# A fused two-layer cross-attention kernel: one engine's order in the first attention, and where the last two batches of the second attention are normalised

## What is computed

```
x = x + att0(layernorm(x), ctx)     # 16 heads of 16; + ctx and a second layernorm inside
x = x + moe(layernorm(x))           # 8 experts, the best 2 of each row, gated, 512 wide
x = x + att1(layernorm(x), ctx)     # 16 heads of 64; 77 text keys with relative positions
x = x + ffn(layernorm(x))           # 8-bit rounded rows, 1024 wide, depthwise convolution of 3

# att1, for one batch:
sim   = (q @ k_text + q @ rel_k[dist]) * scale        # dist = clip(j - i, -16, 16) + 16
attn  = softmax(sim)
out   = attn @ v_text + sum_j attn[i, j] * rel_v[dist[i, j]]
out  += softmax(q @ k_img) @ v_img * (tanh(alpha) + 1) + softmax(q @ k_aud) @ v_aud * (tanh(beta) + 1)
return out @ Wo + bo
```

## Time and profile before

| | |
|---|---|
| median of 3 runs | 952.82 us (952.13 to 952.98) |
| the profiled execution | 951.89 us, of which the span from first to last instruction is 950.1 us |
| busy in the span | PE 862.8 us (91%), PEld 731.4, DVE 604.7 (64%), ACT 465.5, POOL 385.0 |
| mean granted PE clock | 0.974 |
| first attention | 0 to about 204 us |
| experts | about 205 to 430 us |
| second attention | about 430 to 834 us |
| feed-forward | 834.6 to 950 us |

### The profile page before, as it was taken

One profiled execution on the slowest core, in us unless ns is written; L12 is line 12 of the kernel. 1 busy time (PEld: TensorE's weight loads), 2 busy tenths in 40 slices (PEclk: granted clock), 3 DMA queues, 4 the chain that ended last, 5 costly groups with the idle time before them and its releaser, 6 DMA issues. The chain is left out here.

```text
span 950.1 us, 26663 instructions
## 1 busy us (share of the span) xinstructions
PE 862.8 (91%) x9044; PEld 731.4 (77%) x9045; DVE 604.7 (64%) x1484; ACT 465.5 (49%) x1194; POOL 385.0 (41%) x610
## 2 busy tenths in 40 slices
PE   5898988679999999988999899999999999789995
PEld 4777777449999999977465688888888887668774
DVE  3688888555555555542126666878678778459995
ACT  3788888422222222212344445444545454469884
POOL 4488887610000000008002345455555453437662
PEclk9999999989999999999999999999999999889997
DMA  6355557353333333316964777688676866212211
GB/s 166 123 166 169 191 160 237 136 188 102 108 93 99 95 97 95 98 34 227 322 181 137 156 161 174 136 161 180 135 170 141 172 137 126 65 36 64 67 53 45
DMA packets 190187, 128.27 MB, mean 135 GB/s; under 512 B 128544, under 2 KB 175648, under 8 KB 189984
## 3 DMA queue, kind: packets, MB, share of 16 engines
q1 hardware_dynamic: 155728, 93.72, 38.2%
q10 hardware_dynamic: 31312, 25.17, 9.1%
q0 software_dynamic: 3072, 8.39, 2.8%
HBM read 78.25 MB, written 48.99 MB: 134 GB/s over the span
## 5 line engine op out<-in xcount | busy, mean ns | idle before, releaser
L1759 ACT ACTIVATE c_pT<-c_T 128x512 f32<-128x512 f32 (+2 forms) x90 | 50.2, 595 | 104.5 <-PE c_T L1921 73.6
L1702 POOL TENSOR_TENSOR c_soft<-c_soft,c_share 128x616 f32<-128x616 f32 (+2 forms) x96 | 70.4, 761 | 60.9 <-DVE c_share L2177 59.1
L1090 ACT ACTIVATE b_rowsT<-b_RT 128x256 f32<-128x256 f32 x39 | 15.0, 384 | 152.6 <-PE b_RT L1132 152.6
L1712 POOL MEMSET d_round<- 128x1 f32 x1 | 0.1, 98 | 220.9 <-POOLq L977 220.9
L1218 DVE SCALAR_TENSOR_TENSOR b_hidT<-b_U,b_bias,b_gate 128x128 f32<-128x128 f32 x156 | 43.9, 344 | 50.6 <-PE b_U L1141 48.6
L1141 PE MATMUL b_U<-b_rowsT,b_w 128*128 128x128 f32 x624 | 76.0, 275 | 0.0
L1168 PE MATMUL b_Y<-moe_w,b_hidT 128*128 x312 | 73.9, 380 | 0.9 <-DVE b_out L1251 0.9
L1141 PEld LDWEIGHTS b_U<-b_rowsT,b_w 128*128 128x128 f32 x624 | 72.7, 192 | 0.0
L516 ACT ACTIVATE early<-a_S,early 128x128 f32<-128x128 f32 x256 | 70.7, 439 | 4.2 <-DVE early L795 4.2
L2035 PE MATMUL c_O<-early,c_attT 128*128 128x256 f32 x256 | 62.3, 398 | 5.0 <-ACT c_attT L1833 4.4
L1971 PE MATMUL c_T<-c_xT,early 128*128 128x128 f32 x512 | 62.6, 282 | 4.1 <-ACT c_kT L1759 3.6
(11 more groups left out here) (245 smaller groups left out, 2139.9 us busy)
## 6 DMA issues: line engine op xcount, KB each, us to landing
moe_w<-in_L_Wl SPq DMA_DIRECT2D x16, 512.0 KB
rel_windows<-c_relw ACTq DMA_DIRECT2D x28, 276.0 KB, 5.1
c_bias<-rel_windows SPq DMA_DIRECT2D x16, 462.0 KB
prob_rows<-c_soft SPq DMA_DIRECT2D x16, 462.0 KB, 5.1
early<-in_L_early SPq DMA_DIRECT2D x16, 384.0 KB, 3.2
values<-c_pT ACTq DMA_DIRECT2D x22, 256.0 KB, 2.8
first_rows<-expert_lists SPq DMA_DIRECT2D x39, 128.0 KB, 2.5
expert_out<-b_out SPq DMA_DIRECT2D x39, 128.0 KB, 1.7
```

What stands on the lines that cost most here:

```text
L1702: ins = nc.gpsimd.tensor_tensor(soft[p][:, hs, a:z], soft[p][:, hs, a:z], share[:, s, hs].unsqueeze(2).to_broadcast([P, HS, z - a]), ALU.mult)
L1759: nc.scalar.activation(dst, view(T[k]), ACT.Copy, **kw).then_inc(g["emptied"], 1)
```

## The change

```diff
+        norm = weights["Wq"].rearrange("p k (h n) -> p (k h) n", n=P)
...
-        share = sb("c_share", [P, NS, NH])
+        share = [sb(f"c_share{p}", [P, NS, NH]) for p in two]
...
+        def raw(b):
+            return isinstance(b, int) and b >= NB - 2
+
+        def shared_out(b, p):
+            return norm if raw(b) else soft[p]
...
             def prob_out(b, i, p):
-                apart(sp, g["soft"], 2 * b + 2)
+                apart(sp, g["s_exp" if raw(b) else "soft"], 2 * b + 2)
...
                 pool.wait_ge(g["share"], 2 * b + h + 1)
+                if raw(b):
+                    pool.wait_ge(g["pv_mm"], 4 * b)
                 for s, (a, z) in enumerate(STREAMS):
-                    ins = nc.gpsimd.tensor_tensor(soft[p][:, hs, a:z], soft[p][:, hs, a:z],
-                                                  share[:, s, hs].unsqueeze(2).to_broadcast([P, HS, z - a]), ALU.mult)
+                    ins = nc.gpsimd.tensor_tensor(shared_out(b, p)[:, hs, a:z], soft[p][:, hs, a:z],
+                                                  share[p][:, s, hs].unsqueeze(2).to_broadcast([P, HS, z - a]), ALU.mult)
...
+                if last:
+                    pool.wait_ge(s_pin[1 - p], 16 * (b // 2 + 1))
+                    near = band[1 - p][0:NEAR, :, 0:NSTEP - 1]
+                    nc.gpsimd.tensor_tensor(near, near, share[1 - p][0:NEAR, 0, :].unsqueeze(2).to_broadcast([NEAR, NH, NSTEP - 1]), ALU.mult)\
+                        .then_inc(g["steps"], 1)
                 for h in range(2):
                     normalise(b, p, h)
                 tails(b, p)
...
-                else:
+                elif not last:
                     exps(b, p, 1)
                 if not first:
                     bands()
+                if last:
+                    exps(b, p, 1)
...
                 pe.wait_ge(g["bandv"], b + 1)
+                if raw(b):
+                    pe.wait_ge(g["steps"], b - (NB - 2) + 1)
                 pe.wait_ge(s_pin[p], 16 * (i + 1))
...
             ends(NB - 1, 1)
+            dve.wait_ge(s_pin[1], 16 * NPAIR)
+            near = band[1][0:NEAR, :, 0:NSTEP - 1]
+            nc.vector.tensor_tensor(near, near, share[1][0:NEAR, 0, :].unsqueeze(2).to_broadcast([NEAR, NH, NSTEP - 1]), ALU.mult)\
+                .then_inc(g["steps"], 1)
             feed.units(dve, 0, 0)
```

More of the change, by code:

```diff
@@ L894, in steps @@
                     list_rows(b - 4, p)
-                if rows_ready:
-                    rows_normal(b - 3, i - 2 + p, 1 - p)
+                if front:
+                    stats = norm_stats(b + 3, i + 1 + p, 1 - p)
                 if lists:
@@ L899, in steps @@
                 if front:
-                    stats = norm_stats(b + 3, i + 1 + p, 1 - p)
+                    norm_var(stats)
+                if rows_ready:
+                    rows_normal(b - 3, i - 2 + p, 1 - p)
                 if there(b):
                     maxima(b, 0)
-                    maxima(b, 1)
                 if behind:
@@ L906, in steps @@
                     attention_out(den)
[L907 to L910, removed]
+                if there(b):
+                    maxima(b, 1)
                 if behind:
@@ L914, in steps @@
                 if rows_ready:
-                    best = choose_best(best)
+                    best = choose_score(b - 3)
                 if behind:
@@ L918, in steps @@
                 if rows_ready:
+                    best = choose_best(best)
                     best = choose_index(b - 3, 1 - p, best)
@@ L921, in steps @@
                     keys(b + 1, 1 - p)
-                if behind:
-                    rows = rows_scaled(b - 2)
                 if rows_ready:
@@ L926, in steps @@
                 if behind:
+                    rows = rows_scaled(b - 2)
                     rows_out(b - 2, i - 1, p, rows)
@@ L1524, in attention1 @@
         s_x3 = [sem(f"c_x3out{p}") for p in two]
-        names = "filled emptied pick x2 var rstd xn x2b s_mm s_sub s_exp share soft tails bandv pv_mm o_mm o_sb y_mm x3"
+        names = "filled emptied pick x2 var rstd xn x2b s_mm s_sub s_exp share soft tails steps bandv pv_mm o_mm o_sb y_mm x3"
         g = {n: sem("c_" + n) for n in names.split()}
@@ L1708, in tails @@
                 since(pool, g["bandv"], b)
-                nc.gpsimd.tensor_tensor(far[:, :, :], soft[p][:, :, MAXREL:TEXT],
+                nc.gpsimd.tensor_tensor(far[:, :, :], shared_out(b, p)[:, :, MAXREL:TEXT],
                                         cst("behind_band")[:, MAXREL:].unsqueeze(1).to_broadcast([P, NH, TEXT - MAXREL]), ALU.mult).then_inc(g["tails"], 1)
@@ L2000, in probabilities @@
                 pe.wait_ge(g["soft"], 2 * b + k // 2 + 1)
-                return transposes([soft[p][:, 4 * k + j, :] for j in range(4)])
+                return transposes([shared_out(b, p)[:, 4 * k + j, :] for j in range(4)])
             def weighted(b, p, k, n):
@@ L2175, in shares @@
                 since(dve, g["soft"], 2 * b + h - 1)
-                sum_l(nc.vector.reciprocal(share[:, :, hs], total[:, :, hs]))
-                nc.vector.tensor_tensor(share[:, :, hs], share[:, :, hs], coef[:, :, hs], ALU.mult).then_inc(g["share"], 1)
+                sum_l(nc.vector.reciprocal(share[p][:, :, hs], total[:, :, hs]))
+                nc.vector.tensor_tensor(share[p][:, :, hs], share[p][:, :, hs], coef[:, :, hs], ALU.mult).then_inc(g["share"], 1)
                 sum_l.end()
```

## The result

The changed kernel takes 942.02 us (median of 4 runs, 938.43 to 944.5) against 952.9 us for the kernel before (952.13 to 954.03) beside it on the same chip: 0.9882 of it, with a 95% interval of 0.9842 to 0.9922, or 10.9 us less. The forecast was 947.4 us, 5.4 less, with a range down to 944.2. The direction was right, and the gain is twice the forecast and outside its range.

A forecast was written before the change was run, and what follows sets the result against it. It took a ring of waits between DVE and POOL to bound the first attention, and PE's waits for the bands the end. First attention -3.1, trips -1.1 and clock -1.2 gave -5.4: 947.4 us, range 944.2 to 951.0.

The forecast's parts named there:

- The steady steps: First attention, nine steps from batch 3 to 12: POOL allows 0.2 us a step, -1.8 us, bounds 0 and -3.0.
- My two parts of POOL's gain: First attention, each step: the 0.17 us gap ahead of `out_var` shrinks to 0.03; an instruction of 0.38 may fall to 0.21.
- Rival A: First attention: POOL is the bound and its instructions stretch; steady steps give nothing, the phase -0.5; 950.0 us, 18%.
- Start, steps 13 to 15, end: First attention outside the steady steps: start -0.1, steps 13 to 15 -0.8 from POOL's `out_var` wait, end -0.4 from slots.
- The trips: Second attention, batches 14 and 15: earlier raw trips remove PE's 1.17 us wait, -1.1 us; batch 15 at no cost.
- alone, the gain on batch 14 would be given back: Second attention: batch 15's old trip was just in time, so changing only batch 14's would lose its gain there.
- The clock: Second attention, output product of batch 14: from 5.70 to 4.51 us, -1.2 us, bounds 0 and -2.0.
- nothing or all: Output product of batch 14: by the Trainium skill the clock term would be either nothing or all of -2.0 us.
- The turned order of ACT: Second attention: bands go ahead of the second half of the exponentials, which then ends at about 811.8: no cost.
- Rival C: Second attention: the raw trip's first half lands 2 us or more later; only -3.1 stays; 950.7 us, 8%.
- The chance of "faster": Whole kernel: 0.86 for a time below 950.9 us, from all but a tenth of the forecast and parts of the rivals.

The follow-up runs named there:

- e2_trip: The kernel before with only the raw trips of the last two batches and ACT's turned order, first attention as before: 948.39 us, 0.991.
- e3_after: The changed kernel measured again, against the kernel before: 942.51 us, 0.9866.
- e8_actorder: The changed kernel with ACT's last step as it was, second half of the exponentials ahead of the bands: 944.74 us, 0.9925 of the kernel before.
- e1_order: The kernel before with only the new order of the first attention: 947.19 us, 0.9907.
- e6_split: The kernel before with only the maxima split and the scores chosen behind the attended rows, statistics unmoved: 953.4 us, 1.0.
- e4_trip14: The kernel before with the raw trip of batch 14 alone and ACT's turned order, batch 15's trip as before: 955.28 us, 1.0008.
- e9_fillfit: The kernel before with unread PE products: 3 and 2 ahead of the last two bands, 1 ahead of each of the last two output products: 950.93 us, 0.9968.
- e5_stats: The kernel before with only statistics, slots and variance moved ahead of `rows_normal`, maxima in one piece: 947.97 us, 0.9951.

## Why the prediction was right and wrong

**The steady steps** (forecast -1.8, bounds 0 and -3.0): -2.5. The mechanism was right, the size low, because I took one bound for all nine steps. From batch 7 to batch 12 a step took 10.03 to 10.06 us before and 9.81 or 9.82 after: 0.22 to 0.24 less, what I had taken. But from batch 3 to 4, 4 to 5 and 6 to 7 the steps fell by 0.48, 0.39 and 0.39 us. At batch 3 POOL isn't the bound at all. It stood waiting for DVE in the kernel before, so DVE's own gain, which I had at 0.33 to 0.4, arrives. In POOL's timeline before:

```profile
48.67 0.23 POOL L415 TENSOR_SCALAR early<-early 128x1 f32<-128x1 f32 x1 [2.93 <-DVE early L769]
...
108.22 0.20 POOL L439 CAST slots<-a_slot 128x2 int32 x1
```

What set the step from batch 6 to 7 I haven't followed. My two parts of POOL's gain were 0.14 us of idle time and 0.17 for the instruction L415. In the means of five steps from POOL's timelines, counted from the start of one instruction to the start of the next, they were 0.07 (0.15 to 0.08) and 0.12 (0.36 to 0.24). Three changes that I had not seen make up the rest: the first scatter (L434) starts 0.13 us sooner behind `residual`, L442 takes up 0.08 less, and L439 takes up 0.15 more (0.32 us at 114.41 above, 0.20 in the second row here). Together that is 0.24 a step, so the forecast of 0.2 was in part luck. Rival A is out, though L439 did stretch as it said.

**Start, steps 13 to 15, end** (forecast -0.1, -0.8, -0.4). From batch 12's maxima to batch 15's it took 28.20 us before and 28.36 after (28.19 in `e2_trip`, 27.97 in `e3_after`): nothing of the -0.8. I had read POOL's wait of 0.43 us for `out_var` as one that sets the step. `out_var` did come 0.2 us earlier (POOL's instruction 4.21 us behind the maxima of batch 13, 4.40 before). But other things hold `rows_normal`, and with it the next maxima. In the step of batch 13 it is the scatter of an earlier batch, whose transfer still reads the tile that `rows_normal` writes; DVE waited 2.14 us for it, and 1.83 before. In the step of batch 14 it is POOL's next instruction, which waits for `rows_stats` (L839):

```profile
150.02 0.41 DVE L844 TENSOR_SCALAR a_xn<-a_x,early 128x256 f32<-128x256 f32 x1 [2.14 <-DMA expert_lists<-a_xn,a_slot]
150.35 1.28 DVE L795 TENSOR_REDUCE early<-a_S 128x4 f32<-128x512 f32 x2
...
157.56 0.21 POOL L415 TENSOR_SCALAR early<-early 128x1 f32<-128x1 f32 x1 [2.10 <-DVE early L839]
```

The last row is 7.21 us behind the maxima, and was 7.17 before. From the maxima to `rows_stats` DVE does the same instructions in either order and waits for nothing between them (L839 starts 6.94 us behind the maxima, 6.90 before), so nothing can come earlier by turning them round: `rstd1` was ready before DVE asked for it. I had counted a wait of POOL as a gain without asking who waited for POOL.

Five profiled kernels have the old order and five the whole new one, and over them the first attention took 187.9 us against 183.4 in the mean: -4.5 where the sum had -3.1. By parts: from batch 0's maxima to batch 3's -0.8 (27.3 to 28.3 against 26.5 to 28.2), the nine steps -2.5, to batch 15's maxima -0.2, from there to the last places -0.7 (28.5 to 29.4 against 28.0 to 28.4), and behind them -0.3 (12.0 to 13.1 against 12.2 to 12.8). Only in the nine steps and at the end do the two groups stand apart. At the end the wait that I had named, POOL's 0.81 us for the slots, only fell to 0.72 to 0.74, so the -0.7 has another cause, which is not shown. The other parts may be scatter of the clock: between 24 and 28 us the granted clock was 0.64 in the kernel before and 0.85 in `e2_trip`, and with the new order 1.00 in the changed kernel and 0.50 in `e8_actorder`.

**The trips** (forecast -1.1 and no cost). The lengths were right: `prob_out` at 793.21 to `band_in` at 798.27 is 5.1 us (4.9 forecast), POOL's multiplication 1.02 us (1.1) and DVE's 0.66 (0.6). The multiplication of batch 14 was over 1.7 us before PE came (1.9), and that of batch 15 only 0.1 before, where I had 1 us: `ends` waited 2.06 us for POOL's `tails`, a wait that I had not followed. The step that failed is the price of the trip: -1.1 us, the wait of 1.17, where the earlier band was worth 4.3 in the means. I took 1.17 and 0.07 us from one execution, and in that execution the output products of batches 13 and 14, at 4.51 and 5.70 us, had let the trips catch up. For batch 15 the rows were these:

```profile
821.63 0.35 SPq L1599 DMA_DIRECT2D c_band<-prob_rows  x1
...
822.69 1.97 PE L2010 MATMUL c_O<-c_pT,c_v 128*64 128x128 f32 x32
```

The second ends 0.07 us ahead of the band at 824.73, and I read that as a trip without a cost. I put waits and slow products into two separate terms, "-1.1" for the wait and "-1.2" for the clock, as if they added up to the most that was there. But they trade: behind a product at full clock the old trip costs 2.10 us for batch 14 (`e1_order`) and 2.67 for batch 15 (`e6_split`), and 4.20 for batch 15 where batch 14 no longer waits (`e4_trip14`). With nothing but full clock, the 1.17 would have been 1.17 + 0.79 = 1.96, and the row for that, product 13 over product 15, was the earlier trace rows. That "alone, the gain on batch 14 would be given back" holds (`e4_trip14`), and that should have told me that batch 15's margin of 0.07 us was worth a price of its own.

**The clock** (forecast -1.2, bounds 0 and -2.0). In the profiled execution product 14 gave 1.98 and product 15 took 1.61 back. In the means of the tails the slow products shrank by 2.2 us, but that isn't what the clock gave: products 13 and 14 stand ahead of the old band 15, which came no later for them, so only product 15's 0.6 is the clock's. `e9_fillfit` agrees: with both last products at full clock its old tail was as long as that of the kernel before. The term was counted at the wrong product, and what I expected of it came from the trips. I had also worked with "nothing or all" of it by the Trainium skill ("TensorE: Matmul & The Clock Gate", section "What's actually happening"). The section has two levels and no level between, but from that it doesn't follow that a product of several us is wholly at one of them. Here it isn't: the same 16 matmuls took 4.39, 4.83, 5.21 and 5.33 us, and the granted clock over the last of these was 0.69. That the moment varies, as the same section has it, agrees with the runs: in `e3_after` product 13 was the slow one, in the same code profiled before it product 15.

**The sum.** The two lengths together are 4.5 + 5.1 = 9.6 us less; the kernel is 10.9 less, with an interval of 7.4 to 15. Nothing further needs to be found, but nothing that small elsewhere is excluded. The forecast's -5.4 stood against a profiled execution of 951.89 us, near its median, and I took this as a sign that its parts were typical. They were one case of several: `e5_stats` repeats its short waits and slow products, `e1_order` and `e6_split` have long waits. The turned order of ACT I had at "no cost", which holds, but it has a gain that I gave no number: 1.15 us at PE, without which part of the trip's gain goes into a new wait (`e8_actorder`). Three figures of the forecast don't follow from their own terms. Rival C comes to 951.89 - 3.1 + 0.93 = 949.7 us, not 950.7. The chance of "faster" adds up to at most 0.82 from its parts, not 0.86. And the lower end of the range, 944.2, takes in all of the 1.2 us that the bounds of start and end add, not half. None of them changes the outcome.

## What to carry to other kernels

A wait for a transfer that PE reaches after work at half clock is shorter than the wait that is there: price it with that work at its shortest row. Give the clock a term only for work that stands behind the last such wait. Where the last two iterations of a pipeline are both bound by the same trip, shorten both or neither. An idle gap of an engine is a place for its own work that is needed later, but the gain has to be asked for step by step: what ends the wait of the next instruction differed between the first steps, the loop and the last three.

## What the hardware showed beyond that

The same kernel scattered by about 1% from one execution to the next (947.5 to 957.5 us on one chip), and the slower executions tended to have the lower mean granted clock (0.967 to 0.981 there). So gains of one or two microseconds are seen only in the lengths of a stretch, and those of a stretch with the clock at half level only in several traces.

Small instructions of POOL change with DVE's order alone, and both ways: with the new order L415 took 246 ns on average and 286 with the old, while L439 took 328 and 197. With three of the one in a step and one of the other they nearly cancel, so an order that shortens one of them isn't faster for that alone.
